# Attention on one core: the shift rows' transposes move from the score banks into the rotation of the three maxima banks

## What is computed

```python
    def _L1_attn_ref(x, Wq, bq, Wk, bk, Wv, bv, Wo, bo):
        ...
        q = _apply_rope(q, cos, sin)
        k = _apply_rope(k, cos, sin)
        scale = 1.0 / np.sqrt(HD)
        scores = jnp.einsum('bhsd,bhed->bhse', q, k) * scale
        attn = jax.nn.softmax(scores, axis=-1)
        out = jnp.einsum('bhse,bhed->bhsd', attn, v)
        out = out.transpose(0, 2, 1, 3).reshape(b, l, e)
        return out @ Wo.T + bo
```

## Time and profile before

| | |
|---|---|
| median of 3 runs | 1191.84 us (1190.0, 1191.84, 1196.08) |
| profiled execution: span | 1191.5 us |
| TensorE busy | 1039.4 us, 87% |
| VectorE busy | 853.0 us, 72% |
| ScalarE busy | 798.2 us, 67% |
| GpSimd busy | 291.2 us, 24% |
| exponentials, L1339 | 512, 504.2 us |
| maxima reductions, L2044 | 720, 459.8 us |
| copies of shift rows, L1323 | 32, 8.0 us |

### The profile page before, as it was taken

The page is one execution under the profiler, slowest core; times in us unless marked ns, Lnnn a source line. Parts: engine busy times, 40 slices in busy tenths (PEclk is TensorE's granted clock), DMA queues, the critical chain, the costliest instruction groups (busy, mean ns, idle before and its releaser), DMA issues.

```text
span 1191.5 us, 22203 instructions
## 1 busy us (share of the span) xinstructions
PE 1039.4 (87%) x8296; PEld 485.1 (41%) x8300; DVE 853.0 (72%) x1585; ACT 798.2 (67%) x1206; POOL 291.2 (24%) x296
## 2 busy tenths in 40 slices
PE   9936767787989689999999999999999999968795
PEld 6512224786964222222222222222222222448694
DVE  2499997347135689999999999999999992362222
ACT  2653333455545469999999999999999999431122
POOL 0069881655334500000000000000000000026652
PEclk7969998889888879999999999999999999988997
DMA  3056530866642310011100111001110100038683
GB/s 104 1 166 195 179 122 36 260 189 201 186 136 88 122 61 25 12 34 34 34 16 20 34 34 34 9 27 34 34 34 2 33 4 4 4 126 266 204 268 124
DMA packets 49110, 104.16 MB, mean 87 GB/s; under 512 B 9440, under 2 KB 11864, under 8 KB 48620
## 3 DMA queue, kind: packets, MB, share of 16 engines
q1 hardware_dynamic: 43386, 91.76, 24.6%
q0 software_dynamic: 4544, 9.32, 2.4%
q10 hardware_dynamic: 1074, 1.67, 0.4%
HBM read 89.35 MB, written 12.94 MB: 86 GB/s over the span
## 4 chain that ended last, share of the span: by engine, by line
PE 61%; issue 12%; DVE 9%; ACT 9%; DMA 4%; POOL 2%; another core or an unknown queue 1%; SPq 1%; ACTq 0%; DVEq 0%; POOLq 0%
PE psum L966 19%; PE psum L945 12%; PE psum L956 8%; PE psum L1085 6%; PE psum L1096 6%; ACT probs L1339 5%; DVE tile_max L2044 2%; DVE ssm_h L1764 1%; PE psum L789 1%; PE psum L1068 1%; PE psum L769 1%; DMA y_in<-y_dram 1%; ACT ln_xn L1331 1%; POOL h0T L1483 1%
## 5 line engine op out<-in xcount | busy, mean ns | idle before, releaser
L1339 ACT ACTIVATE probs<-psum 128x1024 f32<-128x1024 f32 x512 | 504.2, 1041 | 27.6 <-PE psum L956 22.3
L2044 DVE TENSOR_REDUCE tile_max<-psum 128x1 f32<-128x512 f32 x720 | 459.8, 685 | 31.8 <-PE psum L945 25.1
L945 PE MATMUL psum<-k_stack,q_stack 62*128 62x512 bf16 x994 | 313.3, 388 | 14.1 <-DMA q_stack<-q_dram 8.6
L966 PE MATMUL psum<-probs,v_head 128*32 128x256 f32 (+1 forms) x3840 | 321.0, 406 | 0.6 <-ACT probs L1339 0.4
L956 PE MATMUL psum<-q_stack,k_stack 64*128 64x512 bf16 x1024 | 290.0, 384 | 10.6 <-ACT probs L1339 8.7
L945 PEld LDWEIGHTS psum<-k_stack,q_stack 62*128 62x128 bf16 x994 | 77.4, 94 | 242.7 <-issue 109.7
L966 PEld LDWEIGHTS psum<-probs,v_head 128*32 128x32 f32 x3840 | 75.7, 108 | 164.6 <-issue 126.0
L1535 POOL TENSOR_TENSOR max_parts<-row_max,no_shift 128x8 bf16<-128x8 f32 x32 | 6.4, 200 | 557.0 <-DVE row_max L2020 557.0
L1096 PE MATMUL psum<-w2r,hid 128*128 128x128 f32 x624 | 92.5, 296 | 25.4 <-issue 25.2
L1085 PE MATMUL psum<-x_cols,w1r 128*128 128x128 f32 (+1 forms) x624 | 93.5, 299 | 8.8 <-issue 8.0
L1096 PEld LDWEIGHTS psum<-w2r,hid 128*128 128x128 f32 x624 | 84.3, 210 | 28.0 <-issue 27.6
(11 more groups left out here) (287 smaller groups left out, 1107.5 us busy)
## 6 DMA issues: line engine op xcount, KB each, us to landing
w1r<-w SPq DMA_DIRECT2D x78, 256.0 KB
w2r<-w SPq DMA_DIRECT2D x78, 256.0 KB
ssm_b<-bc_dram SPq DMA_DIRECT2D x32, 512.0 KB, 4.0
k_stack<-k_dram SPq DMA_DIRECT2D x60, 120.0 KB
y_in<-y_dram SPq DMA_DIRECT2D x16, 256.0 KB, 5.1
q_stack<-q_dram SPq DMA_DIRECT2D x30, 96.0 KB
bc_p<-bc_dram SPq DMA_DIRECT2D x5, 512.0 KB, 5.7
xtok_dram<-x_tok SPq DMA_DIRECT2D x8, 256.0 KB, 2.4
```

The costliest lines, as they stand in the source:

```text
L945: mm(bank, queries, k_stack[rows, u, keys:keys + C], start=True, stop=True).then_inc(s1_ps, 1)
L966: i = mm(psum[32 * j:32 * j + VM, 7, lo:hi], v_head[:, u, kt, :], probs[:, kt % 4, j * C + lo:j * C + hi], start=kt == 0, stop=kt == KT - ...
L1339: f(probs[:, kt % 4, hf * HALF:(hf + 1) * HALF], banks(2 * slot, 2), ACT.Exp, scale=SCALE).then_inc(p_ready, 1)
L2044: v.tensor_reduce(top, bank, AX.X, ALU.max).then_inc(s1_read, 1)
```

## The change

It has three parts.

1. The matmul that turns a shift row no longer takes a score slot. It takes a place in the ring of three maxima banks, after the tiles of entry 16 (first half) and of entry 29 (second half). The score slots then alternate by entry alone, 32 places in a head. The first row's matmul stood after entry 17 before. The second stays after entry 29.
2. VectorE copies the rows out (`turn_rows`), between its reads of tile 41 and 42, and between tile 67 and 68. ScalarE no longer does, except for head 0's two rows. SyncE waits for VectorE's copy instead of ScalarE's before it starts the row's transfer.
3. The ring is counted over one list of all tiles and rows (`ring`, `HELD_AT`). A head has 66 places, so it runs on through all heads, also at heads 4, 8 and 12.

GpSimd's two steps now share one semaphore, with the same order.

```diff
-ROWS_AFTER = (8, 14)
+ROWS_AFTER = (2 * KT // 2, 2 * KT - 3)
...
-def bank_of(hs, p):
-    return 4 + (hs % UN + p) % RING if hs else FIRST_BANKS[p % len(FIRST_BANKS)]
+def ring():
+
+    order = []
+    for h in range(NH - 1):
+        for e in range(2 * KT):
+            for p in (2 * (e + LEAD), 2 * (e + LEAD) + 1):
+                order.append(("tile", h + 1 + p // SN, p % SN))
+            if e in ROWS_AFTER:
+                order.append(("row", h + 1, ROWS_AFTER.index(e)))
+    first = [("tile", 1, p) for p in range(2 * LEAD)]
+    return first + [held for held in order if held[1] < NH]
+
+
+HELD = [("tile", 0, p) for p in range(SN)] + ring()
+HELD_AT = {held: i for i, held in enumerate(HELD)}
+
+
+def bank_of(kind, hs, p):
+    return FIRST_BANKS[p % len(FIRST_BANKS)] if hs == 0 else 4 + (HELD_AT[kind, hs, p] - SN + 1) % RING
...
-ENTRIES = 2 * KT + 2
+ENTRIES = 2 * KT
+ISSUED = ENTRIES + 2
...
-        def load_rows(eng, h, u, hf, done):
-            eng.wait_ge(p_ready, done)
+        def load_rows(eng, h, u, hf):
+            if h:
+                eng.wait_ge(rows_turned, 2 * h + (hf - 1))
+            else:
+                eng.wait_ge(p_ready, 3 + hf)
...
-                def row(hs, hf, g, slot):
-
-                    pe.wait_ge(max_parts_ready, hs * 2 + (hf + 3))
-                    pe.wait_ge(p_ready, g + 1)
-                    mm(psum[0:ROWS, 2 * slot, 0:128], max_parts[:, hf].rearrange("p d s j -> p (d s j)"), ident_b[:],
+                def row(hs, hf):
+
+                    pe.wait_ge(max_parts_ready, hs * 4 + (hf * 2 + 4))
+                    if hs:
+                        free(*held_before("row", hs, hf))
+                        bank = bank_of("row", hs, hf)
+                    else:
+                        pe.wait_ge(p_ready, hf + 1)
+                        bank = 2 * hf
+                    mm(psum[0:ROWS, bank, 0:128], max_parts[:, hf].rearrange("p d s j -> p (d s j)"), ident_b[:],
                        start=True, stop=True).then_inc(s2_ps, 1)
...
-                        if following and kt in ROWS_AFTER:
-                            hf = ROWS_AFTER.index(kt)
-                            row(h + 1, hf, h * ENTRIES + (2 + ROW[hf]), ROW[hf] % 2)
...
+                def turn_rows(hs, hf):
+                    dve.wait_ge(s2_ps, (hs - 1) * ISSUED + (issued(ROWS_AFTER[hf], True) + 4))
+                    dve.wait_ge(rows_in[hf], hs * ROW_LOADS)
+                    v.tensor_copy(shift_rows[0:ROWS, hf, :], psum[0:ROWS, bank_of("row", hs, hf), 0:128]).then_inc(rows_turned, 1)
```

More of the change, by code:

```diff
@@ L210, with entry, issued @@
 JOINED_READ = [reads(hs, p + 1) for hs in range(NH) for p in range(SN) if order_of(hs)[p][3] == JOINED]
-ENTRIES = 2 * KT + 2
-def entry(kt, hf, rows=True):
-    return 2 * kt + hf + (rows and sum(kt > after for after in ROWS_AFTER))
-ROW = [entry(after, 1) + 1 for after in ROWS_AFTER]
+ENTRIES = 2 * KT
+ISSUED = ENTRIES + 2
+def entry(kt, hf):
+    return 2 * kt + hf
+def issued(n, rows):
+    return n + (rows and sum(n > after for after in ROWS_AFTER))
 def half_tiles(hf):
@@ L916, in attention, with free @@
                 pe.sem_inc(pv_done, 4)
-                def free(hs, q):
-                    if order_of(hs)[q][3] == APART:
+                def free(kind, hs, q):
+                    if kind == "row":
+                        pe.wait_ge(rows_turned, 2 * hs + (q - 1))
+                    elif order_of(hs)[q][3] == APART:
                         pe.wait_ge(above_ready, joins(hs, q))
@@ L957, in scores, with values @@
                               q_stack[rows, u, hf * C:(hf + 1) * C], start=True, stop=True)
-                def values(h, u, kt, rows, part=None):
+                def values(h, u, kt, part=None):
                     if kt == 0:
@@ L962, in values @@
                         pe.wait_ge(o_copied, h + 1)
-                    pe.wait_ge(p_ready, h * ENTRIES + (entry(kt, 1, rows) + 5))
+                    pe.wait_ge(p_ready, h * ENTRIES + (entry(kt, 1) + 5))
                     lo, hi = (0, C) if part is None else (part * C // 2, (part + 1) * C // 2)
@@ L1330, in above, with exponentials @@
                         act.wait_ge(s1_read, JOINED_READ[n - ABOVE - 1])
-                    f(above_next[n % ABOVE], psum[:, bank_of(hs, p), :], ACT.Relu).then_inc(above_ready, 1)
-                def exponentials(h, kt, hf, rows=True):
-                    n = entry(kt, hf, rows)
+                    f(above_next[n % ABOVE], psum[:, bank_of("tile", hs, p), :], ACT.Relu).then_inc(above_ready, 1)
+                def exponentials(h, kt, hf, rows):
+                    n = entry(kt, hf)
                     slot = n % 2
-                    act.wait_ge(s2_ps, h * ENTRIES + (n + 3))
+                    act.wait_ge(s2_ps, h * ISSUED + (issued(n, rows) + 3))
                     if hf == 0:
@@ L2031, in head @@
                         qt, c, _, kind = order_of(hs)[p]
-                        bank = psum[:, bank_of(hs, p), :]
+                        bank = psum[:, bank_of("tile", hs, p), :]
                         top = (tile_max if hs else first_max)[:, qt, c:c + 1]
@@ L2046, in head @@
                             row_maxima(hs, 0)
+                        for hf in range(2):
+                            of = hs - (2 * (ROWS_AFTER[hf] + LEAD) + 1) // SN
+                            if p == (2 * (ROWS_AFTER[hf] + LEAD) + 1) % SN and of > 0:
+                                turn_rows(of, hf)
                     row_maxima(hs, 1)
```

72 lines of the change are left out of this document (36 added, 36 removed).

## The result

The changed kernel took 1173.14 us in the median of 4 runs, against 1193.96 for the kernel before. The ratio on record is 0.9846, with a 95% interval of 0.9809 to 0.9882. It is not the quotient of the two medians, which is 0.9826. I had predicted 1175.8, with 1170.5 to 1184.0. A second comparison, with 5 runs against 20, gave 1173.04 against 1188.80 and a ratio of 0.9852 (0.9828 to 0.9876).

A forecast was written before the change was run, and what follows sets the result against it. TensorE was taken to set the pace, VectorE close behind, with losses at the shift rows and three ring waits. 8.8 + 3.9 + 0.5 + 2.8 = 16.0 us off the 1191.5 span gave 1175.5, median 1175.8, range 1170.5 to 1184.0.

The forecast's parts named there:

- first row's group: Eight maxima tiles (four entries) around a head's first shift row: 4.56 us instead of 5.15, saving 8.8 us over 15 heads.
- second row's group: Entries 28 to 31, around a head's second shift row: about 4.87 us instead of 5.15, saving 3.9 us over 14 heads.
- ring without a break: At heads 4, 8 and 12 TensorE no longer waits for VectorE over a maxima bank: 3 × 0.93 = 2.8 us off.
- VectorE held by a copy: VectorE's copy of a row from PSUM lasts 0.291 but overlaps by 0.08, so it holds the engine for 0.21 us.
- tile 69's wait: Behind the second row, TensorE's tile 69 waits 0.34 us for VectorE's read of tile 67, said to be delayed by row_max.
- the stretch: Time from the first to the last output copy, heads 1 to 15 almost whole; 554.6 us before the change.
- the first row's matmul being an entry earlier: On TensorE, costs nothing, since its operand depends on tiles up to 33, read about four entries ahead of tile 41.
- ScalarE's idle time: ScalarE's wait in front of an exponential behind a row; the forecast sign was that none remains in the changed profile.
- The late landing: Rival: the second row's transfer lands late, up to 0.31 us wait per head, 4.3 in 14 heads: 1180.1; chance 0.10.
- The free ring: Rival: the ring costs nothing, tile 69 does not wait, saving 0.34 us more in 14 heads: 1171.0; chance 0.12.
- The loss: Rival: time won at the rows returns as bank waits in the groups behind, two thirds gone: about 1187; chance 0.09.
- The hold from which the change loses: Rival: row copies make VectorE the bound; slower once each holds it beyond 0.90 us, 1204 at 1.3; chance 0.04.

## Why the prediction was right, and where not

| step | forecast | measured |
|---|---|---|
| first row's group | 4.56 | 4.55 |
| second row's group | 4.87 | 4.90 |
| ring without a break | 2.8 | 2.8 |
| VectorE held by a copy | 0.21 | 0.20 |
| tile 69's wait | 0.34 | 0.37 |
| a head | 0.87 less | 0.84 less |
| the stretch | 15.2 less | 14.9 less |
| whole kernel | 16.0 less | 15.8 (second set), 20.8 (first) |

**The sum** of the forecast for the stretch is 14 × 0.59 + 13 × 0.28 + 0.5 + 2.8 = 15.2. The measured one is 14 × 0.60 + 13 × 0.25 + 2.8 = 14.5, and 0.4 is left for the last head, where I had 0.5.

**The score slot** was the right place to look. The copy by ScalarE in the ring shows that the engine does not matter: same engine, same copy, the gain stays. But the slots are only 7.3 of the 14.9. The prediction put the first row's matmul being an entry earlier at nothing, and that was so only for its operand. The cheap price that it worked out for this row (0.04 and 0.06) holds for this place alone, and the place is worth 4.8 us.

**The reason for the second row's wait was wrong.** "Tiles 65 to 67 hang on `row_max`" was the step that failed. They hang on the matmul of tile 66. The row of this matmul in the trace of the kernel before:

```profile
728.78 0.39 PE L945 MATMUL psum<-k_stack,q_stack 62*128 62x512 bf16 x1
```

The size came out right by luck, because both ends fall together within 0.04: counted from `row_max` the read of tile 67 ends at 730.45 in the old trace, and counted from tile 66's matmul at 728.78 plus 0.43 plus 0.60 plus 0.68, 730.49. The earlier trace rows could have warned me: its five reads last 3.34, and back to back, as I read them, they would last 4 × 0.60 + 0.68 = 3.08. Moving `row_max` changed nothing, and a first row with no `row_max` near it paid the same 0.37. I should have weighed the two reasons against each other in the rows, for they tell different things about what to change.

**ScalarE's idle time** behind the second row was forecast as gone. It is 0.46, the shadow of tile 69's wait. It costs nothing more by itself. So the forecast sign failed, while the sum held.

**The rivals.** The late landing did not come. Its price was sized too mildly: at 2.36 from the copy to the scores, 0.6 is spare, and one entry less costs 0.5 per head. The 2.0 us that I took from the Trainium skill ("DMA: Bandwidth & Descriptors", Anatomy of one DMA) are stated there for transfers that GpSimd issues. The rows' transfers are issued by SyncE, so that comparison said nothing for or against this rival. The free ring did not come, since the wait of tile 69 is set by TensorE's own pace. The loss did not come back in the groups behind. From entry 20 to 28 TensorE takes 8.9 in each head, again 1.11 per entry. The hold from which the change loses lies between 0.60 (1177.65) and 1.20 (1199.88), and the forecast said 0.90.

**Beyond the attention** nothing was shown to change. The first set's 20.8 us are a difference of two medians of four. The interval of its ratio, 1.2% to 1.9% less, takes in the 16.0 us, so the rest may be scatter of the other stages.

## What to carry to other kernels

When a rare small job shares a double buffer with the main stream, it costs its own turn and makes the next item wait for the one just before it, here 0.69 us for a matmul of 0.15. A longer ring with slack is a better home, and there its place counts: put it where the reader of the ring has the least left to read, and check which wait the second item behind it inherits. Find a stretch between two marks that repeats from run to run and compare variants by it. Here it came out at 539.7 in both profiles of the changed kernel, where the intervals of whole runs reach 2.5 to 5 us to each side.

## What the runs showed of the hardware

Copies of 16x128 from PSUM on VectorE last 0.27 and start 0.20 apart (five in 1.07), reads of 512 columns last 0.68 and start 0.60 apart. Each hides 0.07 to 0.08 of itself under the next. The Trainium skill's rule that I weighed ("VectorE: DVE Perf Modes", The DRAIN you can't avoid) would have them start at their ends, and the trace does not show that. I had left out what the same section adds, that a next operation that is not held starts earlier, and with this the overlap agrees.

The start of head 0's row matmul scatters between profiles although the same instructions stand ahead of it: 409.2 and 416.6 with the old kernel's code there, 408.3 to 418.4 with the changed kernel's. The 540 us of attention behind it, at a granted clock of 1.00, took 539.7 in both profiles of the changed kernel. The start goes with the granted clock of the first 50 us in all fourteen profiles. Where this was 0.93 the matmul came from 408.3 to 409.2 (three profiles), at 0.86 or 0.90 from 410.7 to 412.4 (nine), and at 0.83 at 416.6 and 418.4. That is a pattern, and no run tested whether the clock is the cause.
